# Output projection of an attention kernel: eight block products per head pair replaced by seven, with running sums, on one Trainium2 core

## What is computed

```python
B, S, D = (8, 256, 512)          # the input has 16 batches
H, HD = (16, 128)
q = (inputs_q @ Wq).reshape(b, sq, H, HD) * (1.0 / np.sqrt(HD))
k = (inputs_kv @ Wk).reshape(b, skv, H, HD)
v = (inputs_kv @ Wv).reshape(b, skv, H, HD)
attn = jax.nn.softmax(jnp.einsum('bqhd,bkhd->bhqk', q, k), axis=-1)
ctx = jnp.einsum('bhqk,bkhd->bqhd', attn, v).reshape(b, sq, H * HD)
...
x = x + _L0_xattn_ref(_layernorm(x, axis=-1), ctx_2048, Wq, Wk, Wv, Wo)      # ctx @ Wo
x = x + _L0_ffn_ref(_layernorm(x, axis=-1), w_gate, w_up, w_down)
# ffn: q(q(silu(q(x)@q(w_gate).T) * (q(x)@q(w_up).T)) @ q(w_down).T)
```

## Time and profile before

| | |
|---|---|
| three runs | 2032.74, 2033.76 (median), 2034.96 us |
| the profiled execution, its own time | 2033.7 us |
| its span, first to last instruction | 2032.1 us |
| granted TensorE clock, mean | 1.0 of full speed |
| PE / PEld busy | 2015.9 / 1509.0 us |
| DVE / ACT / POOL busy | 1528.7 / 1001.7 / 733.0 us |

### The profile page before, as it was taken

The page is one execution under the profiler, slowest core; times in us unless marked ns, Lnnn a source line. Parts: engine busy times, 40 slices in busy tenths (PEclk is TensorE's granted clock), DMA queues, the critical chain, the costliest instruction groups (busy, mean ns, idle before and its releaser), DMA issues.

```text
span 2032.1 us, 44899 instructions
## 1 busy us (share of the span) xinstructions
PE 2015.9 (99%) x15422; PEld 1509.0 (74%) x15422; DVE 1528.7 (75%) x3346; ACT 1001.7 (49%) x2679; POOL 733.0 (36%) x872
## 2 busy tenths in 40 slices
PE   8999999999999999999999999999999999999999
PEld 6888888788888887878888888888888885444444
DVE  6767777777777777777787777776666557899886
ACT  8955554554555545554555555554555443333332
POOL 5422232332333233333332323322111104877776
PEclk9999999999999999999999999999999999999999
DMA  8834444444444444444444343534332364555555
GB/s 255 217 65 90 83 97 87 84 92 92 88 88 91 92 91 86 88 89 91 89 89 92 77 105 73 104 74 91 55 82 58 68 136 97 91 89 94 92 91 99
DMA packets 456112, 193.75 MB, mean 95 GB/s; under 512 B 419456, under 2 KB 432256, under 8 KB 455904
## 3 DMA queue, kind: packets, MB, share of 16 engines
q1 hardware_dynamic: 433984, 140.31, 36.2%
q0 software_dynamic: 15584, 44.45, 8.8%
q10 hardware_dynamic: 6336, 6.29, 1.0%
HBM read 61.21 MB, written 27.26 MB: 44 GB/s over the span
## 4 chain that ended last, share of the span: by engine, by line
PE 93%; DVE 2%; DMA 2%; ACT 2%; issue 1%; DVEq 0%; SPq 0%; POOL 0%; ACTq 0%; POOLq 0%
PE b_qk L1103 33%; PE b_v L1103 17%; PE b_c L1103 10%; PE b_s L1103 9%; PE b_w L1158 8%; PE b_o L1158 8%; PE b_o L1229 3%; PE b_w L1229 2%; PE b_x L1103 2%; PE b_pt L1103 2%; DMA probT<-psplit 1%; DMA attn_weights<-wattn 0%; ACT psplit L665 0%; DVE nmax L919 0%; ACT prob L655 0%
## 5 line engine op out<-in xcount | busy, mean ns | idle before, releaser
L1103 PE MATMUL b_qk<-kvT,attn_weights 128*128 128x256 f16 x3072 | 377.2, 273 | 3.5 <-DVE qk L757 2.5
L1103 PE MATMUL b_qk<-xT,attn_weights 128*128 128x256 f16 x3072 | 377.2, 273 | 0.0
L1103 PE MATMUL b_v<-attn_weights,kvT 128*128 128x256 f16 x3072 | 377.2, 273 | 0.0
L655 ACT ACTIVATE prob<-b_s,nmax 128x256 f32<-128x256 f32 x514 | 239.2, 470 | 274.8 <-DVE nmax L919 272.8
L1103 PEld LDWEIGHTS b_qk<-kvT,attn_weights 128*128 128x128 f16 x3072 | 300.3, 98 | 92.5 <-issue 3.5
L946 DVE SCALAR_TENSOR_TENSOR psplit<-prob,rrec,psplit 128x256 f16<-128x256 f32 x514 | 307.1, 638 | 79.1 <-ACT psplit L665 79.1
L611 ACT ACTIVATE qk<-b_qk 128x512 f16<-128x512 f32 x256 | 152.5, 596 | 428.1 <-PE b_qk L1103 428.0
L757 DVE SCALAR_TENSOR_TENSOR qk<-b_qk,qk 128x512 f16<-128x512 f32 x256 | 176.7, 690 | 247.7 <-ACT qk L611 240.0
L1103 PEld LDWEIGHTS b_qk<-xT,attn_weights 128*128 128x128 f16 x3072 | 300.6, 98 | 34.8
L1103 PEld LDWEIGHTS b_v<-attn_weights,kvT 128*128 128x128 f16 x3072 | 300.6, 98 | 34.8
L665 ACT ACTIVATE psplit<-prob,rrec 128x256 f16<-128x256 f32 x514 | 233.1, 500 | 67.5 <-DVE rrec L939 67.5
(11 more groups left out here) (137 smaller groups left out, 2678.4 us busy)
## 6 DMA issues: line engine op xcount, KB each, us to landing
ffn_w<-wffn SPq DMA_DIRECT2D x48, 256.0 KB, 2.9
acc<-xtok POOLq DMA_DIRECT2D x16, 512.0 KB, 4.7
out<-acc POOLq DMA_DIRECT2D x16, 512.0 KB, 3.3
xrow<-xtok POOLq DMA_DIRECT2D x31, 256.0 KB, 3.2
...
```

The costliest lines, as they stand in the source:

```text
L655: last = eng.activation(half(prob, q, 256), half(bS, q, 256), ACT.Exp, bias=nmax[:, q:q + 1], scale=1.0, accum_out=rsum[:, q:q + 1])
L1103: last = eng.matmul(out, l, r, start=(a == 0), stop=(a == len(pairs) - 1))
```

## The change

**Seven products.** The output of a head pair (two 128x128 blocks of context rows by two 128x256 halves of weights for each head) is computed by seven products of block sums. Names: `a0`, `a1` are the first and second 128 rows of one head's context, `b0`, `b1` those of the other. `TERMS` lists the seven, which sum of context blocks they take and which block of prepared weights. They go to four PSUM banks: `m1`, `m3` in `b_pt`, `m4`, `m2` in `b_x`, `m5`, `m7` in `b_o`, `m6` in `b_w`. Each is three matmuls over 256 columns, 21 in place of 12 over 512. Batches 0 and 1 keep the old way (`FAST = 2`), batches 2 to 15 take the new one: 14 batches of 8 pairs, 112 pairs.

**Context sums.** ACT writes the context as float32 into `blocks` (a view of `cbuf`), `evict_rows`, and DVE's low part of the context goes. Once per pair POOL makes the sums (`left_sums`, three operations of 256, 256 and 128 columns), ACT the high part (`left_hi`, 896 columns), DVE the low part (`left_lo`, 896 columns, into `stage`).

**Weight sums.** In batch 1 POOL, ACT and DVE make the seven weight blocks of each of the eight pairs (`out_sums`, `out_hi`, `out_sums_hi`, `out_lo`), and they are stored to `out_scratch` in DRAM. In batches 2 to 15 two pairs' weights stay in SBUF, the other six go through two slots, loaded by SP's queue in two parts of 128 partitions by 2048 and 1536 float16 (`load_slot`, `fill`). The feed-forward weights' quantising starts one batch later (`FFN_FROM`).

**Sums to the rows.** At a batch's end DVE adds 12 pieces of 128x256 to `acc` in place of two of 128x512: four in each of the heads `k` 1, 2 and 3 of the next batch's first quad (`add_products`). Each first product of the next batch waits for the sums that read its bank (`m_step`, `READ`).

**The rest.** Of the root for the rows POOL does only the power (`tile_power`), DVE the rest (`x1_root`). The feed-forward stage uses two pairs of banks up to product 28, then three, `NO_DOWN` has ten entries in place of eight, and the last batch's 12 sums are one per pair `v`.

```diff
+FAST = 2
+FAST_PAIR, FAST_HEAD = 8 * FAST, 16 * FAST
+RESIDENT = {0: 0, 4: 1}
+RING = {1: 2, 2: 3, 3: 2, 5: 3, 6: 2, 7: 3}
+PART_COLS = (2048, 1536)
+LEFT = {"a0": 0, "b1": 1, "a0+b1": 2, "a0+b0": 3, "a1+b1": 4, "b0-b1": 5, "a0-a1": 6}
+TERMS = (("m1", "a0+b1", 3), ("m3", "a0", 2), ("m4", "b1", 1), ("m2", "a1+b1", 0)), \
+    (("m6", "a0-a1", 5), ("m5", "a0+b0", 4), ("m7", "b0-b1", 6))
+READ = {"m1": 4, "m3": 4, "m4": 8, "m2": 8, "m6": 9, "m5": 12, "m7": 12}
-NO_DOWN = (0, 1, 2, 3, 36, 40, 44, 48)
+NO_DOWN = (0, 1, 2, 3, 44, 47, 50, 53, 56, 59)
-GU_BUF = [u % 2 if u < 4 else (u - 2) % 3 for u in range(2 * PAIRS)]
+GU_BUF = [u % 2 if u < THIRD else (u - THIRD + 2) % 3 for u in range(2 * PAIRS)]
...
# SP
+            def load_slot(u, part):
+                slot, _ = slot_use(u)
+                at = slot * 3584 + part * PART_COLS[0]
+                eng.wait_ge(sm["wo_stored"], 16 * (PREP.index(u % 8) + 1))
+                eng.dma_start(oall[:, at:at + PART_COLS[part]],
+                              wos[u % 8, :, part * PART_COLS[0]:part * PART_COLS[0] + PART_COLS[part]]
+                              ).then_inc(sm[f"slot_loaded{slot}{part}"], 16)
...
# POOL
+            def left_sums(n, k):
+                wait_apart(eng, "c_hi", 4 * n + k + 1)
...
+                eng.tensor_tensor(blocks[:, 4:6, :], blocks[:, 1:9:7, :], blocks[:, 0:4:2, :], ALU.add
+                                  ).then_inc(sm["s_sum"], 1)
+                eng.tensor_tensor(blocks[:, 6:8, :], blocks[:, 0:2, :], blocks[:, 2:9:6, :], ALU.subtract
+                                  ).then_inc(sm["s_sum"], 1)
+                eng.tensor_tensor(blocks[:, 3, :], blocks[:, 1, :], blocks[:, 2, :], ALU.add).then_inc(sm["s_sum"], 1)
...
# ACT
+            def evict_rows(n, k):
+                i = 4 * n + k
+                eng.wait_ge(sm["c_done"], i + 1)
...
+                at = blocks[:, 1:9:7, :] if k % 2 else blocks[:, 0:4:2, :]
+                eng.activation(at, bC[:, 0:256].rearrange("p (q f) -> p q f", q=2), ACT.Copy, scale=C_OUT
+                               ).then_inc(sm["c_hi"], 1)
+            def left_hi(n, k):
+                u = 2 * n + k // 2 - 2 - FAST_PAIR
+                eng.wait_ge(sm["s_sum"], 3 * (u + 1))
...
# DVE
+            def left_lo(n, k):
+                eng.wait_ge(sm["s_hi"], 2 * n + k // 2 - 1 - FAST_PAIR)
+                eng.tensor_tensor(left_part(k // 2, 1).rearrange("p (n f) -> p n f", f=P), blocks[:, 1:8, :],
+                                  left_part(k // 2, 0).rearrange("p (n f) -> p n f", f=P), ALU.subtract
+                                  ).then_inc(sm["s_lo"], 1)
+            def add_products(b, group):
+                if group == 0:
+                    eng.wait_ge(sm["o_done"], 16 * b + 15)
+                    eng.wait_ge(sm["acc_loaded"], 16 * (b + 1))
+                    add_product(b, "m1", 1, 0, 0, None)
+                    add_product(b, "m1", 1, 1, 1, None)
+                    add_product(b, "m3", -1, 0, 1, None)
+                    add_product(b, "m3", -1, 1, 1, 2)
+                if group == 1:
...
+                if group == 2:
+                    eng.wait_ge(sm["o_done"], 16 * b + 16)
+                    add_product(b, "m6", -1, 1, 1, 7)
+                    add_product(b, "m5", -1, 0, 0, 5)
+                    add_product(b, "m5", 1, 0, 1, 3)
+                    add_product(b, "m7", 1, 0, 0, 10)
...
# PE
+            def project_fast(u, part):
...
+                eng.wait_ge(sm[f"slot_loaded{slot}{part}"], 16 * use)
+                if part == 0:
+                    eng.wait_ge(sm["s_lo"], u - FAST_PAIR + 1)
...
+                for name, rows, block_ in TERMS[part]:
+                    at = LEFT[rows] * P
+                    if first_ and batch > FAST:
+                        eng.wait_ge(sm["m_step"], 12 * (batch - 1 - FAST) + READ[name])
+                    for z, (a, b) in enumerate(PARTS):
+                        last = eng.matmul(product_at[name], left_part(u % 2, a)[:, at:at + P], slot_w(slot, block_, b),
+                                          start=(first_ and z == 0 and name in OPENS), stop=(last_ and z == len(PARTS) - 1 and name in CLOSES))
+                last.then_inc(sm["o_done"], 1)
```

456 lines of the change are left out of this document (307 added, 149 removed).

## The result

The changed kernel takes 2044.6 us in the median of 5 runs (2042.72 to 2046.19), against 2033.87 us (2032.74 to 2034.96): a ratio of 1.0052, 95% interval 1.0038 to 1.0067. It is slower, by 10.7 us. 2020.8 was forecast, with a range of 2001 to 2038.

A forecast was written before the change was run, and what follows sets the result against it. PE's own work was taken to bound the kernel. From 2033.7 us, -34.4 for shorter products, +12.1, +5, +3.4 and +1 for new waits gave -12.9, so 2020.8 us, with a range of 2001 to 2038.

The forecast's parts named there:

- shorter products: In PE's output product, 21 matmuls of 256 columns replace 12 of 512, saving 0.307 us a pair: -34.4 us.
- border sums: At 13 batch borders, PE's first products wait 0.30 and 0.63 us for DVE's sums behind `nmax`: +12.1 us.
- preparation in batch 1: Preparing the weights in batch 1 costs nothing; without cover, up to 1 us for each of 8 pieces.
- DMAs: Slot loads, 12 per batch, raise the DMA share to 0.65 and may delay transposes: +1 us, ends 0 and 25.
- Term 2: In the quads where rows are normalised, DVE comes late for `qk` and PE waits: +5 us, ends 0 and 17.
- term 3: Step into the feed-forward stage: new waits behind the last head and with two bank pairs, +3.4 us, ends 1 and 7.
- L: How late DVE comes for `qk` in a head, in us; PE feels it from about 2.1.
- The prediction's own sign of being wrong: PE waits on `qk` or `probT` above 1 us a batch, or the sums' waits missing.
- DVE becomes the bound over a third of the batch: Rival: term 2 at its upper end, 17, and DVE late by 0.3 at each border, 2037 us; chance 0.12.
- The rival on the slow side, late transposes: At the context product, transposes share engines with slot loads and come late, two waits a batch: 2070 us; chance 0.18.

The follow-up runs named there:

- e2: Changed kernel with the low part of the seven left-side blocks (`left_lo`) covering 14 columns in place of 896: 2021.1 us.
- e15: Changed kernel with three of GpSimd's four feed-forward rounding operations covering only 8 columns: 2023.3 us.
- e1: Changed kernel with batch 1's weight-preparing arithmetic over 8 columns a piece in place of 256 and 512, loads and stores kept: 2038.1 us.
- e11: Changed kernel with slots of prepared weights reloaded, after their first filling, with one row of 128: 2040.6 us.
- e4: Changed kernel with each of the twelve sums into `acc` per batch covering 8 columns in place of 256: 2026.9 us.
- e7: Changed kernel, nothing left out, with the border's twelve sums in heads k = 1 and 2 and `ffn_y` one head later: 2028.4 us.
- e14: Changed kernel, nothing left out, with batch 1's next load issued ahead of the last piece's store: 2041.4 us.
- e6: Changed kernel, nothing left out, with batch 1's preparing arithmetic on ScalarE and VectorE moved, store and load half a head later: 2057.9 us.
- e9: e6 with GpSimd's root and normalising in batch 1 put ahead of the sums that wait for the load: 2054.5 us.
- e5: Kernel before the change, with only two pairs of feed-forward banks until product 28, the third behind it: 2035.5 us.
- e12: e7 with ScalarE's second silu and VectorE's second inner ahead of the last pair's `left_hi` and `left_lo`: 2025.9 us.

## Why the prediction was wrong

| term | forecast | measured | read from |
|---|---|---|---|
| shorter products | -34.4 | -33.6 | 112 x (13.07 - 12.77) |
| border sums | +12.1 | +12.7 | 13 x (103.15 - 102.17), e2 and e15 |
| DVE late | +5 | +22.1 | batches 3 to 13: 1153.4 - 11 x 103.15 = 18.8; batch 2: 105.28 - 102.02 (e2), of which 0.5 to 0.7 in its first head is the preparation's |
| step into the feed-forward stage | +3.4 | +6.9 | 359.1 - 352.8, and 0.6 of shorter products there |
| preparation in batch 1 | 0 | +5.1 | 109.68 - 104.56, e1 |
| DMAs | +1 | within the rows above | 4.0 at most by e11 |

Together +13.2. The kernel before had 3.2 us of stalls in batches 2 to 8 that are not counted in these terms, and the changed one has 0.7 more at its start. What is left to +12.3, the difference of the spans, is 1.6 us in batch 15, where the late transposes' two named waits are 1.57.

- **The shorter products and the border were right.** 21 matmuls at 0.109 us, and 0.30 and 0.63 us of wait forecast, 0.32 and 0.65 measured. e4 and e7 show that it is these sums, and that the wait was a choice of place.
- **Term 2 failed, and it alone turned the sign.** Put at 22.1 in place of 5, it gives some +4 us against before, about 2038, still at the edge of the range; the preparation and term 3 carried the time out of it. Its bound was right: late by 2.1 forecast, about 2.0 shown. The step that failed is the lateness at which the sum for head 10 starts. "0.7 + 0.5 + 1.1 gives L near 2.2" (the three make 2.3) took the 0.7 from the trace of before, where head 10 itself began on time (+3.45). After the change head 10 begins 0.7 late. Head 8's `left_lo` hands 0.85 to head 9, and head 9, 0.3 shorter than before and now with the statistics (1.28 + 0.25 + 0.16 us), gives back only 0.15 of it. With `left_lo` narrow and the statistics in the same place heads 9 and 10 are on time (run 2). Whether the statistics elsewhere would be enough, no run tells. 2.3 and this 0.7 are 3.0, and 3.0 was measured. Above the bound each tenth costs a tenth in every batch: 1.1 us at head 11, and what stayed late made heads 13, 0 and 1 wait for 0.5 more. That is 1.7 us a batch where 0.4 was taken and 1.4 was the upper end. The prediction's own sign of being wrong, over 1 us a batch of PE waiting for `qk`, came: 12.8 us are named in batches 2 to 13.
- **The preparation failed.** It was costed at nothing because "feed-forward quantising has left that batch's DVE ... ACT is at half load", which counts busy shares; up to 1 us for each of 8 pieces was named for the case that this cover is gone. What bound it is a loop through one buffer, 13.8 us against the 13.1 of two heads. e1 shortens it by its arithmetic and the wait goes; e14 by its load, half goes, and the store's landing takes over; e6 and e9 lengthened it (a load's landing takes up to 8.1 us there, 6.3 in the change) and cost 13 and 10 us. Only the four together show that it is the loop; a second buffer, which would cut it, wasn't tried.
- **Term 3 was mis-sized by 3.5 us.** Two pairs of banks cost 1.7 by e5's trace, where 3.3 less the 0.8 of before were forecast. Of the rest the trace names waits of 0.56 for `cbuf` and 1.01 for `left_lo`, and 1.3 us more than before stand behind PE's last matmul (4.5 against 3.2). The wait for `inner` was not mended by e12, and no run divides this further.
- **The DMAs were right in kind**: 12 loads per batch, the share at 0.62, seven named waits, 3.8 us.
- **The rivals.** "DVE becomes the bound over a third of the batch", 2037, named the cause, with too small a price: 17 us for term 2, 5 too low, and nothing for the preparation. The rival on the slow side, late transposes, came true only at the end of batch 15, with 1.6 us.
